# Attention heads in a macaron block: groups of three steps, scores four steps ahead, six places of exponentials

## The reference

```python
q_lat = (x @ Wq_down).reshape(b, t, H, L)          # H = 16 heads
...
q = jnp.concatenate([q_c, _apply_rope(q_e, cos, sin)], axis=-1)
k = jnp.concatenate([k_c, _apply_rope(k_e, cos, sin)], axis=-1)
scores = jnp.einsum('bhqd,bhkd->bhqk', q, k) * scale   # 16 numbers a head
scores = jnp.where(causal[None, None], scores, -jnp.inf)
att = jax.nn.softmax(scores, axis=-1)
y = jnp.einsum('bhqk,bhkd->bhqd', att, v)
```

## Time and profile before

| | us |
|---|---|
| runs: median (lowest to highest) of 3 | 1198.94 (1198.63 to 1202.97) |
| the profiled execution's own time | 1200.27 |
| its span, first to last instruction | 1198.5 |
| the heads stage in it, first maxima to last copy | 451 to 886 |
| busy: TensorE | 994.5 (83%) |
| busy: VectorE | 766.0 (64%) |
| busy: ScalarE | 674.8 (56%) |
| busy: GpSimd | 508.0 (42%) |

### The profile page before, as it was taken

How to read it: one execution, slowest core, us unless ns; L and a number is a source line. 1 busy time by engine, 2 the same in 40 slices (tenths; PEclk the granted TensorE clock), 3 DMA queues, 4 the chain that set the end, 5 groups by cost and what they waited for, 6 DMA issues and landing times. The chain is left out here.

```text
span 1198.5 us, 25179 instructions
## 1 busy us (share of the span) xinstructions
PE 994.5 (83%) x9046; PEld 726.2 (61%) x9046; DVE 766.0 (64%) x1557; ACT 674.8 (56%) x1595; POOL 508.0 (42%) x692
## 2 busy tenths in 40 slices
PE   5227999999789958999999999999978399999930
PEld 1125778878778844555555555555546278888830
DVE  3894444444377637788888888888717844444437
ACT  2733445444357522777787777878747645555410
POOL 1525667766445540222332323323220067777710
PEclk9658999999589985899999999999989589999965
DMA  8723655553447554245464544535129523333349
GB/s 306 242 85 103 209 184 192 203 177 141 157 139 243 173 166 82 72 102 116 108 139 96 126 109 103 116 94 122 42 59 348 166 83 104 103 104 105 101 136 316
DMA packets 100582, 172.94 MB, mean 144 GB/s; under 512 B 16240, under 2 KB 64368, under 8 KB 100464
## 3 DMA queue, kind: packets, MB, share of 16 engines
q1 hardware_dynamic: 86640, 133.57, 38.9%
q0 software_dynamic: 13824, 37.77, 9.2%
HBM read 101.55 MB, written 69.47 MB: 143 GB/s over the span
## 5 line engine op out<-in xcount | busy, mean ns | idle before, releaser
L1827 ACT ACTIVATE spare<-h_psS 128x512 f32<-128x512 f32 x576 | 306.8, 601 | 94.2 <-PE h_psS L1737 91.8
L1855 DVE TENSOR_REDUCE h_part<-h_psM 128x2 f32<-128x1024 f32 (+3 forms) x256 | 249.1, 1015 | 13.1 <-PE h_psM L1716 12.5
L1890 POOL TENSOR_SCALAR_AFFINE_SELECT spare<-spare 128x256 f32<-128x256 f32 x256 | 99.5, 407 | 306.5 <-ACT spare L1827 306.5
L899 PE MATMUL m_psG<-wgu,m_x_hi 128*128 x576 | 194.8, 420 | 1.2 <-DVE m_x_lo L973 1.2
L877 POOL DMA_INDIRECT ys<-m_y,m_slot_u x144 | 142.2, 988 | 77.8 <-ACT m_y L964 55.1
L1764 PE MATMUL h_psO<-spare,a_VP 128*17 128x256 f32 (+3 forms) x3072 | 166.1, 335 | 9.7 <-ACT spare L1818 8.7
L1716 PE MATMUL h_psM<-h_KT,h_QT 48*128 48x512 f32 (+3 forms) x768 | 147.9, 427 | 22.5 <-DMA h_QT<-a_QD 15.0
L1737 PE MATMUL h_psS<-h_QT,h_KT 49*128 49x512 f32 (+3 forms) x768 | 158.5, 407 | 3.7 <-ACT spare L1827 2.7
L871 POOL DMA_INDIRECT m_xg<-xn,m_slot_u x140 | 135.6, 969 | 47.9 <-issue 22.6
L983 DVE TENSOR_TENSOR m_h<-m_act_g,m_psG 128x256 f32<-128x256 f32 x144 | 60.6, 421 | 136.0 <-ACT m_act_g L957 131.4
L899 PE MATMUL m_psY<-wdn,m_h_hi 128*128 x576 | 128.3, 304 | 10.4 <-issue 5.9
(11 more groups left out here) (230 smaller groups left out, 1574.6 us busy)
## 6 DMA issues: line engine op xcount, KB each, us to landing
xn<-spare SPq DMA_DIRECT2D x16, 512.0 KB, 5.8
wg_d<-wgu SPq DMA_DIRECT2D x16, 512.0 KB
p_yg<-ys SPq DMA_DIRECT2D x16, 512.0 KB, 5.3
a_KD<-spare SPq DMA_DIRECT2D x32, 256.0 KB, 2.9
h_KT<-a_KD SPq DMA_DIRECT2D x64, 128.0 KB
h_QT<-a_QD SPq DMA_DIRECT2D x64, 128.0 KB
a_OD<-spare SPq DMA_DIRECT2D x128, 64.0 KB, 2.5
wgu<-wg_d SPq DMA_DIRECT2D x16, 512.0 KB, 10.6
```

Of the source, the lines that this page charges most:

```text
L899: m = pe.matmul(out, s[:, c, :], ww[:, bass.ds(at + c * width, width)], start=(n == 0), stop=(n == 3 * CC - 1))
L1827: act.activation(prob[k % NP][:, h, :], psS[x % NS][:, :], ACT.Exp).then_inc(s_read, 1)
L1855: m = dve.tensor_reduce(out, psM[k % NM][:, :, at:at + n], AX.X, ALU.max, negate=True)
L1890: m = pool.affine_select(block, block, [[0, 2], [1, P]], ALU.is_ge, 0.0, 0, -1)
```

## The change

In `Order` the groups become three of three steps instead of four of two and one of one. In `heads` there are six places for exponentials instead of five (NP), and scores run four steps ahead instead of three (LAG). The copy of a pair's results stands behind the exponentials of step 1 of the next pair (OUT) instead of step 2. In a group of three TensorE now issues: the first scores, the three values, the second scores, the maxima that go with the first and the second, the third scores, and the maxima that go with these.

```diff
     PER = 9
-    TOGETHER = ((0, 1), (2, 3), (4, 5), (6, 7), (8,))
+    TOGETHER = ((0, 1, 2), (3, 4, 5), (6, 7, 8))
+    OUT = 1
...
-    Q, K3, NM, NS, NP, NK, LAG = P // 2, 3 * DH, 2, 3, 5, 4, 3
+    Q, K3, NM, NS, NP, NK, LAG = P // 2, 3 * DH, 2, 3, 6, 4, 4
...
                         for k in ks:
                             values(k)
-                        for k in new[1:]:
+                        for k in new[1:2]:
                             scores(k)
-                        for k in new:
+                        for k in new[0:2]:
+                            ahead(k)
+                        for k in new[2:]:
+                            scores(k)
                             ahead(k)
...
-                    if i == LAG - 1 and p >= 1:
+                    if i == order.OUT and p >= 1:
                         out(p - 1)
```

## The result

The changed kernel takes **1246.57 us** (median of 4, 1245.13 to 1247.50), the kernel before 1198.79 beside it: ratio **1.039, 95% interval 1.0356 to 1.0424**, so 48 us slower. The forecast of slower was right, 1230 was 16.6 us too low, and 1246.6 lies outside the range of 1217 to 1243.

A forecast was written before the change was run, and what follows sets the result against it. It took VectorE's reductions, holding the third maxima of each group, to bound the new order: 13.75 against 12.50 us a pair, 29 x 1.25 = 36.3 less 5.5 for reciprocals, +30.8 us, so 1230 us, range 1217 to 1243.

The forecast's parts named there:

- Maxima c wait for the reduction of a: In each group of three, the third maxima wait for VectorE's reduction of the first, as maxima have only two banks.
- The wait for the copy: Next pair's first values wait for the copy of the results; the change was to save 0.35 us a pair.
- the reciprocal is swallowed: VectorE's idle 0.8 us in each group was to hide the reciprocal: 0.78 x 7 = 5.5 us gained.
- TensorE's stops: Pauses of TensorE before maxima, released by VectorE: 0.7 to 0.9 us, three times a pair.
- Rival 1: TensorE's runs of values decide, so fewer runs make the change faster: 1171 us; chance 0.04.
- Together 13.75 us a pair: Sum of the loops in the three groups of a pair, 4.29, 4.98 and 4.48 us, against 12.50 before.
- after values 0 to 2: Loop of the group with the turned row and maxima in two parts: 4.98 us.
- The turned row: TensorE's extra row (L1745) in the group after values 0 to 2, priced 0.20 us; bounds 0 to 0.4.
- after values 3 to 5: Loop of the group with plain maxima: 4.29 us, including 0.41 for the group's first scores.
- after values 6 to 8: Loop of a pair's last group, with its third maxima in two parts: 4.48 us, including 0.05 for the bank's release.
- the clock: Two short falls of TensorE's granted clock, each about 1.4 us, may go or double: -3 to +3 us.
- Rival 3: TensorE's pauses bring more clock falls, one in every second pair, 14 x 1.4: 1250 us; chance 0.06.

The follow-up runs named there:

- e11: Kernel before with TensorE's order rewritten, six runs of values a pair, scores three steps ahead, and VectorE's reciprocal three steps later in its queue: ratio 0.9915 to before.
- e10: Kernel before with interleaved order, seven runs of values a pair, scores four ahead, copy behind step 1, reciprocal three steps later: ratio 0.9932 to before.
- c1: The changed kernel run once more as a control, on other chips of the same kind: ratio 1.0385 to before.
- e13: Kernel before, order untouched, with the reciprocal two steps earlier in VectorE's queue, where the denominators' transfer has not landed: ratio 1.0288 to before.
- e12: e9 with the reciprocal three steps later in VectorE's queue: ratio 0.9909 to before.
- e9: Kernel before with TensorE's order rewritten, six runs of values a pair, scores four steps ahead, copy behind step 3: ratio 1.0099 to before.
- e3: Changed kernel whose VectorE reductions read only half of the columns: ratio 1.012 to before, one run; plain pair 13.08 us.

## Why the prediction was right in kind and short in size

**Right.** Maxima c wait for the reduction of a; 94 of these stops stand in the trace. The wait for the copy is gone, the reciprocal is swallowed, ScalarE idles 34 us more (30 forecast). The signs were met less exactly than the kind of loop: the plain pair is above the 13.6 to 13.9 named, and TensorE's stops are 0.4 to 0.7 us in the matmuls' records, not 0.7 to 0.9. Rival 1 fell: fewer runs brought nothing. The Trainium skill's rule that switching modes drains TensorE (TensorEngine Tiling (Array Packing), Key Properties) agrees with the tail of 0.12 us after every run of values; it isn't what decides, as e11 with six runs a pair and e10 with seven beat before with five.

**The step that failed**, first part, is the size of the loop: "Together 13.75 us a pair", measured 14.04, so 29 x 0.29 = 8.4 us. Alone it would have left the result inside the range, at 1238. Group by group:

- after values 0 to 2: 4.98 forecast, 543.72 - 538.53 = 5.19 measured. The turned row costs 539.29 - 538.53 - 0.34 = 0.42, not 0.20. I took its price from where it stood next to values, where TensorE changes shape anyway; between scores and maxima it brings two changes of its own. 0.4 was my upper bound, and the value taken should have been that one.
- after values 3 to 5: 4.29, measured 547.92 - 543.72 = 4.20. Scores A took 0.33, not 0.41, ahead of values.
- after values 6 to 8: 4.48, measured 4.65 (the remainder of 14.04). Scores A follow maxima c after 0.54, not 0.47 (550.38 to 550.92). And the bank comes free later: in the pair before, b's reduction starts at 536.11, 0.08 ahead of the end of a's as its pitch of 1.14 says, and c at 536.35, so 0.16 after that end, not 0.05:

```profile
536.11 1.22 DVE L1859 TENSOR_REDUCE h_part<-h_psM 128x2 f32<-128x1024 f32 x1
...
536.35 0.33 PE L1717 MATMUL h_psM<-h_KT,h_QT 48*128 48x128 f32 x2 [0.69 <-DVE h_part L1859]
```

(VectorE's row of b, TensorE's of c.) In this group c is a pair's first maxima, which also wait for K and Q; whether that second wait is the 0.1 wasn't tried.

**The step that failed, second part**, is a term that the sum put at nothing: the clock. I held its falls to be worth -3 to +3 and left more of them to a rival of 0.06. They gave +5.9 in pairs 1 to 29. The low clock in pairs 30 and 31, which I had left at nothing, gave most of +3.2: with 10.2 us at half clock this stretch takes 25.5 us, in c1, with 3.4, 23.2. That stops bring falls is shown by e13 against before (6 to 2) and e12 against e9 (0 to 5), where only the place of the reciprocal differs. For the changed kernel it rests on e3: the same order, its waits for VectorE down to 0.2 us and less in the matmuls' records, has none in one execution, the changed kernel six and three in two. How many falls a given stop brings stays open. Rival 3 named the right cause and 1250 us, near the 1246.6, but by one fall in every second pair, 20 us; its number is near by luck.

The forecast was +30.8 us and the spans differ by 47.1. So 8.4 + 5.9 + 3.2 of the missing 16.3 are named. What remains is +1.9 at the start of the stage, -1.2 of small differences in the pairs, and -2.0 in the rest of the program, of which I know no cause.

## What to carry to other kernels

When work of several engines is written out by hand into one engine's queue, add up the loop through each pair of buffers (issue, fill, read, release, and all that stands in the queue until the next issue): batching three steps was to save 0.38 us of changes of shape and made the pair 1.5 us longer. About 1.0 of it went when VectorE, which with two buffers can't run ahead across the batch, was relieved; then the scores' banks were next. Spread the work that fills the scarce buffers between the long runs. The orders found so, with a reciprocal that no longer stands in the queue ahead of its transfer, took 0.9% off the kernel before; the share of each was not measured alone. Price a moved block by its new neighbours.

## What the hardware showed that I had not expected

A wait of 1 to 2 us on VectorE, which stops TensorE behind it, can cost far more than itself. In e13 seven waits of 1.8 us on average, behind which TensorE stands still for 2.4 to 3.3 us, cost 36 us, as the granted clock fell to half of its 2.4 GHz for 3.4 to 17 us at a time beside six of them; a fall of 3.4 us costs 1.5 us. Stops of 0.4 to 0.7 us three times a pair came with three to six falls in 29 pairs. The Trainium skill (TensorE: Matmul & The Clock Gate, HAM oscillation — how this bites in real kernels) tells of idle gaps of TensorE that throttle it again and again. The runs agree: e13's gaps of 2.4 to 3.3 us recur only every fourth pair, and in e9 falls came behind gaps as short as 0.5 us.
